# Causal attention stage: 24 steps a sequence in place of 32, a second copy of the rows by transfers, and weights turned by products with the identity

## The reference, cut to what matters

```python
dot = einsum('bhid,bhjd->bhij', q, k)                      # 16 heads, 16 features each
vals = sum(q*q, -1, keepdims=True) + sum(k*k, -1, keepdims=True).transpose(0, 1, 3, 2)
scores = dot * dot / (vals - 2.0 * dot + EPSILON)
scores = scores + triu(ones((Lq, Lq)), k=1) * -1e9
out = einsum('bhij,bhjd->bhid', softmax(scores), v)        # then @ w_out + b_out
```

## Time and profile before

| | us |
|---|---|
| median of 3 runs | 5136.44 |
| lowest, highest | 5132.15, 5155.20 |
| profiled execution, whole | 5161.38 |
| profiled execution, span | 5159.0 |
| PE, DVE, ACT, POOL busy in the span | 4558.8, 3311.3, 2661.4, 2321.9 |

### The profile page before, as it was taken

How to read it: one execution, slowest core, us unless ns; L and a number is a source line. 1 busy time by engine, 2 the same in 40 slices (tenths; PEclk the granted TensorE clock), 3 DMA queues, 4 the chain that set the end, 5 groups by cost and what they waited for, 6 DMA issues and landing times.

```text
span 5159.0 us, 74358 instructions
## 1 busy us (share of the span) xinstructions
PE 4558.8 (88%) x26848; PEld 2760.8 (54%) x26848; DVE 3311.3 (64%) x7776; ACT 2661.4 (52%) x5897; POOL 2321.9 (45%) x2331
## 2 busy tenths in 40 slices
PE   7888888999999999997888888878899999999997
PEld 3444445555555555555555455545555555555564
DVE  4454566666666666647877787778666666656653
ACT  4443444444444444338778777777544444444442
POOL 1111144454554545335555555565544545445441
PEclk9999999999999999987887787778899999999998
DMA  2000000000000000000000000000000000100000
GB/s 64 9 5 5 26 5 11 3 5 3 20 9 24 9 11 7 22 10 1 6 5 5 1 10 5 18 1 5 26 5 3 5 19 4 30 11 17 15 17 19
DMA packets 51004, 61.32 MB, mean 12 GB/s; under 512 B 11848, under 2 KB 43216, under 8 KB 50640
## 3 DMA queue, kind: packets, MB, share of 16 engines
q1 hardware_dynamic: 50640, 56.58, 3.5%
HBM read 35.61 MB, written 12.58 MB: 9 GB/s over the span
## 4 chain that ended last, share of the span: by engine, by line
PE 66%; DVE 16%; ACT 6%; issue 6%; POOL 4%; DMA 1%; SPq 1%; DVEq 0%; POOLq 0%; ACTq 0%
PE wide L692 46%; PE o_ps L692 9%; PE wide L695 5%; PE turn_ps L695 5%; PE turn_ps L692 2%; DVE prob L1231 2%; DVE x_n L1107 1%; DMA shifted<-resid 1%; DVE w_down L1220 1%; POOL w_up L1418 1%; DVE pt L1257 1%; DVE st L1238 1%; POOL rn L1401 1%; ACT pt L1070 1%; SPq L1459 1%
## 5 line engine op out<-in xcount | busy, mean ns | idle before, releaser
L1431 POOL TENSOR_SCALAR prob<-prob,st 128x256 f32<-128x256 f32 (+1 forms) x1024 | 524.0, 531 | 979.2 <-DVE st L1244 979.1
L692 PE MATMUL wide<-w_in,x_t 128*128 128x512 f32 (+1 forms) x1792 | 826.0, 606 | 2.8 <-DVE w_up L1205 1.5
L692 PE MATMUL o_ps<-pt,v 128*64 128x256 f32 (+2 forms) x5632 | 640.0, 373 | 194.8 <-DVE pt L1257 101.8
L692 PE MATMUL wide<-x_t,w_up 128*128 128x512 f32 (+1 forms) x1536 | 696.1, 599 | 15.7 <-DVE k_t L1167 11.4
L1070 ACT ACTIVATE pt<-turn_ps 128x512 f32<-128x512 f32 x384 | 229.2, 597 | 864.5 <-PE turn_ps L695 864.4
L692 PEld LDWEIGHTS o_ps<-pt,v 128*64 128x64 f32 (+1 forms) x5632 | 393.4, 141 | 465.8 <-issue 208.1
L695 PE MATMUL turn_ps<-ident,prob 128*128 128x128 f32 x2816 | 466.6, 285 | 126.5 <-ACT pt L1070 121.3
L1039 ACT ACTIVATE prob<-prob,st 128x256 f32<-128x256 f32 (+1 forms) x1024 | 478.9, 472 | 188.8 <-DVE st L1231 188.6
L695 PEld LDWEIGHTS turn_ps<-ident,prob 128*128 128x128 f32 x2816 | 315.5, 142 | 421.1 <-issue 240.3
L692 PEld LDWEIGHTS wide<-w_in,x_t 128*128 128x128 f32 x1792 | 337.6, 198 | 361.8 <-issue 356.3
L692 PEld LDWEIGHTS wide<-x_t,w_up 128*128 128x128 f32 (+1 forms) x1536 | 259.6, 178 | 366.5 <-issue 346.6
(11 more groups left out here) (137 smaller groups left out, 8111.8 us busy)
## 6 DMA issues: line engine op xcount, KB each, us to landing
kept<-resid SPq DMA_DIRECT2D x16, 512.0 KB, 2.6
x_n<-kept SPq DMA_DIRECT2D x16, 512.0 KB, 3.2
shifted<-resid SPq DMA_DIRECT2D x32, 224.0 KB
w_in<-in_f_wqkv SPq DMA_DIRECT2D x4, 1536.0 KB, 7.0
w_up<-in_f_w SPq DMA_DIRECT2D x4, 1364.0 KB, 6.0
resid<-in_x SPq DMA_DIRECT2D x8, 512.0 KB, 8.4
out<-resid SPq DMA_DIRECT2D x8, 512.0 KB, 2.9
w_down<-in_f_w SPq DMA_DIRECT2D x4, 640.0 KB
```

The costliest lines, as they stand in the source:

```text
L692: return eng.matmul(out, lhsT, rhs, start=start, stop=stop, skip_group_check=True)
L1431: last = eng.tensor_scalar(pr[:, local_span(t)], pr[:, local_span(t)], sm[:, 8 + t:9 + t], 1.0, ALU.mult, ALU.mult)
```

## The change

Step kinds: a pair of heads now takes three steps, with the tiles (1, 0), (2) and (3), so 3, 3 and 4 blocks a head; 24 steps a unit. The first kind puts the two blocks of tile 1 and the one of tile 0 side by side. The number of blocks is the same.

Rows: bk and bq turn 128 columns at once by a true transpose, four heads a group, four groups a unit. So q_rows and k_rows hold four heads once each. Two new parts on SP, dup_a and dup_b, copy 64 of the 128 rows by transfers to the other half of q_half and k_half; the denominator's products read q_rows and k_rows, the numerator's q_half and k_half at the other 64 partitions. turn_a and turn_b become products with the identity as the moving operand. Rooms of b_den and b_inv are cut to make place for q_half and k_half, and the planner's costs are changed.

```diff
-BSTEPS = GROUPS * 4 * 2
+B_TILES = [(1, 0), (2,), (3,)]
+BSTEPS = BHEADS // 2 * len(B_TILES)
+def b_blocks(i):
+    out, at = [], 0
+    for t in B_TILES[i % 3]:
+        out.append((t, at, P * (t + 1)))
+        at += P * (t + 1)
+    return out
...
-B_COST = {"bclip": (0.15, 0.27), "bnum": (0.1, 0.22), "bguess": (0.2, 0.47), "bclose": (0.2, 0.6), "bmul": (0.5, 0.63),
-          "exp": (0.45, 0.26), "turn_a": (0.05, 0.16), "turn_b": (0.05, 0.16), "pt_a": (0.06, 0.12),
-          "pt_b": (0.12, 0.135), "mix": (0.1, 0.28), "mask": (0.85, 0.0)}
+B_COST = {"bclip": (0.15, 0.27), "bnum": (0.1, 0.22), "bguess": (0.2, 0.47), "bclose": (0.2, 0.6), "bmul": (0.8, 0.6),
+          "exp": (0.85, 0.21), "turn_a": (0.03, 0.28), "turn_b": (0.03, 0.28), "pt_a": (0.06, 0.12),
+          "pt_b": (0.12, 0.135), "mix": (0.05, 0.28), "mask": (0.95, 0.0)}
...
-        b_den = [w_up_room[:, 1024 * i:1024 * i + 1024] for i in range(3)]
-        b_inv = [x_t2[:, :, :].rearrange("p c n -> p (c n)"), x_n2[:, :, :].rearrange("p t f -> p (t f)"),
-                 b_hid[:, 2048:3072]]
+        b_den = [w_up_room[:, 0:768], w_up_room[:, 768:1536], w_up_room[:, 1536:2560]]
+        b_inv = [x_2[:, 0:768], x_2[:, 768:1536], b_hid[:, 2048:3072]]
+        q_half, k_half = w_up_room[:, 2560:3072], x_2[:, 1536:2048]
...
                     for t in range(TILES):
-                        for r in range(4):
-                            at = t * P + BROW * (2 * (i % 2) + r // 2)
-                            last = mm(turn_ps[r * BROW:(r + 1) * BROW, t * P:(t + 1) * P], src[:, i // 2, at:at + BROW],
-                                      ident[:, :], True, True)
+                        last = tr(turn_ps[:, t * P:(t + 1) * P], src[:, i, t * P:(t + 1) * P])
...
-                    for what in ("bden", "bdot"):
-                        for k in range(2):
-                            r = 2 * BROW * k + (BROW if what == "bdot" else 0)
+                    dup = "dup_b" if half else "dup_a"
+                    pe.wait_ge(S[dup], 32 * nth(dup, u, g))
+                    for t, at, n in b_blocks(i):
+                        for what in ("bden", "bdot"):
+                            for k in range(2):
+                                r = 2 * BROW * (half if what == "bden" else 1 - half) + BROW * k
+                                q_in, k_in = (q_rows[g % 2], k_rows[g % 2]) if what == "bden" else (q_half, k_half)
...
-                    at, to = (0, 0) if kind == "turn_a" else (P * (i % 4 + 1), 512)
-                    for kb in range(i % 4 + 1):
-                        last = tr(ps[:, to + kb * P:to + (kb + 1) * P],
-                                  prob[SLOTS[u, i]["prob"]][:, at + kb * P:at + (kb + 1) * P])
+                    at, to = (0, 0) if kind == "turn_a" else (b_width(i), 512)
+                    for kb in range(b_width(i) // P):
+                        last = mm(ps[:, to + kb * P:to + (kb + 1) * P],
+                                  prob[SLOTS[u, i]["prob"]][:, at + kb * P:at + (kb + 1) * P], ident[:, :], True, True)
...
+                elif kind in ("dup_a", "dup_b"):
+                    half = 0 if kind == "dup_a" else 1
+                    here, there = slice(64 * half, 64 * half + 64), slice(64 - 64 * half, 128 - 64 * half)
+                    sp.wait_ge(S["bk_c"], nth("bk_c", u, i))
+                    sp.wait_ge(S["bq_c"], nth("bq_c", u, i))
+                    if i:
+                        sp.wait_ge(S["bdot"], nth("bdot", u, 6 * (i - 1) + 3 * half + 2))
...
+                    dma(q_half[there, :], q_rows[i % 2][here, :]).then_inc(S[kind], 16)
+                    dma(k_half[there, :], k_rows[i % 2][here, :]).then_inc(S[kind], 16)
```

More of the change, by code:

```diff
@@ L228, in parts_of @@
         if st == "b":
-            g = k // 4
-            if k % 4 == 0:
+            g = k // 6
+            dup = "dup_a" if k % 6 < 3 else "dup_b"
+            if k % 6 == 0:
                 for kind in ("bk", "bq"):
                     put(kind, g, at - 4 / steps, final("brow", 3))
-                    free = (u, 4 * (g - 1) - 1) if g >= 2 else (u - 1, 4 * (g + 7) - 1)
+                    free = (u, 6 * (g - 1) - 1) if g >= 2 else (u - 1, 6 * (g + 3) - 1)
                     put(kind + "_c", g, at - 4 / steps, final(kind, g), ("bdot", *free), ("down", u - 1, 3))
+                for half in range(2):
+                    free = (u, 6 * (g - 1) + 3 * half + 2) if g else (u - 1, 18 + 3 * half + 2)
+                    put("dup_b" if half else "dup_a", g, at - 3 / steps, final("bk_c", g), final("bq_c", g), ("bdot", *free),
+                        ("down", u - 1, 3), ("back", u - 1, 0))
             last = ("bdot", u, k - 1) if k else ("bdot", u - 1, steps - 1)
-            put("bden", k, at, final("bk_c", g), final("bq_c", g), last, *turned, ("down", u - 1, 3))
-            put("bdot", k, at, final("bk_c", g), final("bq_c", g), final("bden", k))
+            put("bden", k, at, final("bk_c", g), final("bq_c", g), final(dup, g), last, *turned, ("down", u - 1, 3))
+            put("bdot", k, at, final("bk_c", g), final("bq_c", g), final("bden", k), final(dup, g))
             three = (u, k - 3) if k >= 3 else (u - 1, k + steps - 3)
@@ L677, in halves, with b_rows, own, blocks @@
             return a.rearrange("p (h u e) -> p h u e", u=2, e=HD // 2)
+        def b_rows(i):
+            return [slice(k * b_width(i) + at, k * b_width(i) + at + n) for k in range(2) for t, at, n in b_blocks(i)]
+        def own(a, i):
+            a = a.rearrange("p (k n) -> p k n", k=2)
+            return a[:, :, P:3 * P] if i % 3 == 0 else a[:, :, b_width(i) - P:b_width(i)]
+        def blocks(a):
+            return a.rearrange("p (c n) -> p c n", n=P)
         def two(a, n):
@@ L815, in tensor_program @@
                 elif kind == "bdot":
-                    g, t = i // 4, i % 4
+                    g, half = i // 6, i // 3 % 2
                     pe.wait_ge(S["bk_c"], nth("bk_c", u, g))
                     pe.wait_ge(S["bq_c"], nth("bq_c", u, g))
-                    for what in ("bden", "bdot"):
-                        for k in range(2):
-                            r = 2 * BROW * k + (BROW if what == "bdot" else 0)
[L822 to L825, removed]
+                    dup = "dup_b" if half else "dup_a"
@@ L1013, in scalar_program @@
                 elif kind == "bnum":
-                    w = P * (i % 4 + 1)
+                    w = b_width(i)
                     exp_tables()
```

120 lines of the change are left out of this document (72 added, 48 removed).

## The result

| | before | changed |
|---|---|---|
| median of 16 runs each, us | 5136.87 | 5109.67 |
| lowest, highest | 5119.59, 5167.18 | 5096.82, 5123.09 |
| ratio, 95% interval | | 0.9935 [0.992, 0.9949] |
| profiled span | 5159.0 | 5114.0 |

The change is faster by 0.65%, some 33 us by the ratio (the medians lie 27 apart), where 79 were forecast: the right sign, about two fifths of the size. By stretches (start and end, length, busy us of PE, PEld, DVE, ACT, POOL, each with its count, then granted clock, share of the transfer engines and GB/s) the causal stage now reads

What follows compares the result with a forecast made beforehand. No engine was saturated; in a loop of engines PE was late most often, partly through its clock. DVE 130.5 plus 26.5 idle made 157.0 us a unit, -10.3 x 8 + 3 = -79, so 5057 us; range 4987 to 5163.

Steps and rivals of the forecast that it cites:

- DVE's term: VectorE's busy time in a causal unit: 131.9 - 1.4 = 130.5 us, making it the fullest engine.
- Steps: 24 steps a causal unit in place of 32, each keeping 1.1 us of DVE idle time: 26.5 us, from 35.4.
- Eight equal units: Causal stage taken as about eight repeating units, each going from 167.3 to 157.0 us, -10.3 a unit.
- The clock: PE's granted clock in the causal stage rises from 0.80 to 0.95, ends 0.72 and 0.99.
- The product: One product with the identity in the weights' turns costs PE 0.26 us, 41.6 us a unit for 160.
- rival B: In turn_a and turn_b, a product costs 0.44 us; unit 178 us, kernel slower at 5227 us; chance 0.11.
- the clock pays it back: A higher PE clock makes up the net +8.8 us a unit of PE work at full clock.
- ACT and the rows: ACT falls from 131.4 to 120 us a unit; PE loses 16.2 us of rows' products, gains 4.2 of transposes.
- Transfers: 16 copies of 128 KB a unit stay hidden behind three steps, some 20 us; 3 us once in the first unit.
- rival D: Copies not hidden, late by half a landing each, +10 us a unit: 5137 us; chance 0.10.
- Rival A: PE's clock stays at 0.80, busy 147 us, unit 170 us: +27 us, 5163 us; chance 0.14.
- C: Clock holds and pipeline tightens to 148 us a unit, DVE's waits for PE nearly vanishing: 4987 us; chance 0.12.

Runs made afterwards that it cites:

- e7: Changed kernel with two GpSimd products (Newton step, mask) replaced by powers on a few columns, about as long: 0.957 of the kernel before.
- e6: Kernel before with GpSimd's products of the Newton step and mask replaced by powers on 2 to 12 columns, about as long: 0.9803 of the kernel before.
- e10: e9 with the planner's bmul cost raised from (0.8, 0.6) to (1.0, 0.85): 0.9831 of the kernel before, median 5069.6 us.
- e3: 24 steps a unit with their planner costs, rows made as before without transfers, transposes for the weights: 1.006 of the kernel before.
- e4: Kernel before with only the weights' transposes turned into products with the identity: 1.0076 of the kernel before.
- e11: e5 with products in place of transposes for the weights, 32 steps kept: 0.9949 of the kernel before.
- e2: Changed kernel with the weights turned by transposes again, order of work unchanged: 0.9904 of the kernel before, median 5095.3 us.
- e14: e7 with transposes for the weights in place of products: 0.9504 of the kernel before, median 4905.7 us.
- e1: The changed kernel itself, run again as the yardstick: 0.9939 of the kernel before, median 5111.3 us.
- e5: Kernel before with only the rows by true transposes and second copies by transfers, their planner costs, fewer b_den and b_inv rooms: 0.9934 of the kernel before.
- e8: Changed kernel without all second copies of the rows but the first two, so products read stale rows: 0.9952 of the kernel before.
- e9: e2 with the planner's cost of the turns put back to (0.05, 0.16): 0.9869 of the kernel before, median 5092.1 us.
- e13: Changed kernel, products kept, with the planner's bmul cost raised from (0.8, 0.6) to (1.0, 0.85): 0.9928 of the kernel before.

## Why the prediction was wrong, point by point

**The failed step is DVE's term**, "DVE 131.9 - 1.4 = 130.5, the middle". It counted instructions and their fixed part and took their lengths as given. Measured: 137.0 in a regular unit, and 84.5 us more over the run where eight units with 1.4 less would be 11 less. Without GpSimd's traffic the term comes out about right (112.7 against 114.0), but the lengths of bmul's maxima depend on GpSimd: 39.9 us a unit became 52.1. With 130.5 and the measured idle time of 23.4 the unit would be 153.9 by the prediction's own sum. The rows ahead of the prediction held no form of DVE at all, and the same view of the kernel before had the warning in it: its L1220 over 512 columns alone lies between 679 and 1751 ns. e7 and e6 show the cause. They do not show that each microsecond of DVE is one of the kernel: e10 has a busier DVE than the changed kernel and is faster.

**Steps.** "If a step keeps 1.1 us, 24 steps have 26.5": measured 23.4. Right in size, but the sum of both was 160.4 and not 157.0, 3.4 us a regular unit. e3 shows that the steps alone cost 0.6%.

**Eight equal units.** The prediction took eight units like the two that it read. They are not alike. The seven distances between the output projections of the causal units sum to 1209.8 us before and 1145.3 after, -64.5, which is near the -72 forecast for seven, and near it by luck: the first five give -26.9 where -51.5 was forecast, and the last two, 190.5 and 182.8 us before and 167.8 and 168.0 after, give -37.5 where -20.6 was.

**The clock.** "I take 0.95": measured 0.85, and 0.93 once VectorE was free (e7). Up in direction, short in size. That the products raise it is shown by e4 (0.80 to about 0.9) and e11 (0.72 to 0.89). What the forecast missed is that a higher clock did not shorten the kernel: e2 and e14 have lower clocks, the same regular unit and no longer time.

**The product.** 0.26 forecast, 0.23 to 0.26 measured; rival B's 0.44 is out. But "the clock pays it back" is not borne out in any of four pairs. In the two within one group the products lose 0.35% (e1 against e2) and 0.8% (e4 against before). In the two across groups (e11 against e5, e7 against e14) the difference has the same sign and is about the size of the spread between groups. Of the two pages of the Trainium skill weighed in the prediction, "Perfetto Trace Analysis", section "Transposes", which says to use the transpose, gives the faster kernel here (e2 against e1). "TensorE: Matmul & The Clock Gate", Part 4, on transposes and the clock, is in line with the clock of 0.91 with products against 0.80 with transposes (e4).

**ACT and the rows.** ACT 120 forecast, 122.9 measured. Rows: of the 37.0 us of PE work that go, 16.2 are the rows' products, and 4.2 us of transposes come in; that part alone is worth as much as the whole change (e5).

**Transfers.** Hidden, as forecast (e8); rival D falls. The first scores come at 2303.67 in place of 2299.47 us, 3.5 of it because the add before them ends later; the 0.7 us that PE waits there for a copy are the transfers' part, 3 forecast.

**The two edges of the stage.** With -64.5 between the projections the span moved by -45 only, for the stretch ahead of the first projection is 11.8 us longer and the one behind the last 7.7 (5.1 and 4.1 in the changed kernel's second profile). And the profiled execution of before was 24 us above its median, that of the changed kernel 6. The front edge goes with the same failed term: DVE is busy 146.0 us there in place of 129.0, and without the traffic the changed kernel reaches its first projection 17.9 us earlier than the kernel before (2444.3 in e7, 2462.2 in e6). The end does not: it is 7.7 us longer in e7 than in e6 as well, and why stays open.

Rival A (clock stays, 5163) and C (4987) did not come. C needed DVE's idle time to halve to 17.7 us a unit beside 130.5 busy; e7's short unit is another thing, for it has 112.7 busy and 27.2 idle.

## What to carry to other kernels

Before a step of VectorE is priced, look at the shortest and the longest of its instruction: where they differ by more than twice on one shape, price it by what GpSimd does beside it. Making steps longer saves fixed parts and lengthens the overlaps. A higher granted clock is not a gain by itself: here one higher by 0.07 to 0.17, bought by 16 to 20 us of PE work a unit, made no kernel faster. And a cost in the plan is worth a trial at the measured time of the engine that is held up: it gave 0.4% with transposes (e9 to e10) and nothing with products (e13).

## What the runs showed of the hardware that I had not expected

A VectorE maximum over 384 columns with both inputs in SBUF takes 0.56 us, and in the changed kernel 2.68 where a GpSimd product over 1024 columns (2.36 us) started 0.09 us ahead of it; what it loses is about the rest of the other instruction. But beside a GpSimd power on 3 to 12 columns that runs 0.8 to 2.8 us, the maxima over 128 to 512 columns take 0.28 to 0.69 us in the middle of their range, which is what they take with GpSimd idle (e7), though that instruction reads and writes SBUF too. So what holds VectorE up in these runs is GpSimd's wide products and not its being busy. The clock stood at 0.72 over whole units in which PE was busy 132 of 160 us (e5), and at 0.89 in the same kernel with products in place of transposes (e11).
